# Attention and a routed feed-forward layer on one core: the last stage begins with the first chunk's norms, turn and routing ahead of the next chunks' work

## The reference

```python
def _L0_ffn_ref(x, Wr, br, W1, b1, W2, b2):
    scores0 = x[:, 0, :] @ Wr + br
    _, idx = jax.lax.top_k(scores0, k)
    W1g, b1g = (W1[idx], b1[idx])
    W2g, b2g = (W2[idx], b2[idx])
    h = jnp.einsum('bsd,bkde->bkse', x, W1g) + b1g[:, :, None, :]
    h = jax.nn.gelu(h, approximate=False)
    o = jnp.einsum('bkse,bkef->bksf', h, W2g) + b2g[:, :, None, :]
    return jnp.sum(o, axis=1) / k
x = L0_attn_x
x = x + _layernorm(_L0_attn_ref(_layernorm(x, axis=-1), ...), axis=-1)
x = x + _layernorm(_L0_ffn_ref(_layernorm(x, axis=-1), ...), axis=-1)
```

## Time and profile before

| | us |
|---|---|
| median of 3 runs | 2064.71 |
| lowest and highest run | 2061.21, 2065.99 |
| the profiled execution, its own time | 2067.85 |
| its span, first to last instruction | 2066.1 |
| stage C within the span | from 1706 to 2066.1 |
| busy over the span: PE, DVE, ACT, POOL | 1978.9, 1799.9, 1362.3, 316.4 |

### The profile page before, as it was taken

One profiled execution on the slowest core, in us unless ns is written; L12 is line 12 of the kernel. 1 busy time (PEld: TensorE's weight loads), 2 busy tenths in 40 slices (PEclk: granted clock), 3 DMA queues, 4 the chain that ended last, 5 costly groups with the idle time before them and its releaser, 6 DMA issues.

```text
span 2066.1 us, 39584 instructions
## 1 busy us (share of the span) xinstructions
PE 1978.9 (96%) x15700; PEld 863.7 (42%) x15700; DVE 1799.9 (87%) x3564; ACT 1362.3 (66%) x1651; POOL 316.4 (15%) x366
## 2 busy tenths in 40 slices
PE   6999999999999999999999999999999996999997
PEld 3655333333333333333333333333333324666664
DVE  6876799999999999999999999999899917899873
ACT  3766657777777777777777777777777781333332
POOL 5333201010110101011100101011010104322000
PEclk9999989999999999999999999999999998999998
DMA  4877613150504224030513314050422034453220
GB/s 124 254 242 207 156 26 67 28 90 8 89 18 85 47 48 82 16 89 13 85 32 68 71 26 89 7 90 20 82 48 50 17 104 108 123 148 108 82 67 31
DMA packets 144651, 162.40 MB, mean 79 GB/s; under 512 B 52690, under 2 KB 118354, under 8 KB 144466
## 3 DMA queue, kind: packets, MB, share of 16 engines
q1 hardware_dynamic: 137554, 147.26, 30.5%
q0 software_dynamic: 6912, 12.61, 2.7%
HBM read 99.77 MB, written 59.77 MB: 77 GB/s over the span
## 4 chain that ended last, share of the span: by engine, by line
PE 79%; DVE 13%; ACT 4%; issue 1%; SPq 1%; DMA 1%; POOL 0%; ACTq 0%; DVEq 0%; POOLq 0%
PE b_psO L1103 25%; PE b_psS L1086 25%; PE b_ring L605 13%; PE a_psQK L888 6%; DVE b_pmax L621 3%; PE a_psV L900 3%; PE c_psH L1483 3%; PE c_psO L1496 2%; ACT b_prob L1050 2%; PE b_ring L603 1%; DVE c_attn L105 1%; DVE c_ln_f_stats L81 1%; DVE c_ln_x_stats L81 1%; PE c_psA L1453 1%; DVE c_x L1314 1%
## 5 line engine op out<-in xcount | busy, mean ns | idle before, releaser
L621 DVE TENSOR_REDUCE b_pmax<-b_ring 128x1 f32<-128x512 f32 (+4 forms) x2284 | 1336.6, 647 | 82.1 <-PE b_ring L605 65.1
L1050 ACT ACTIVATE b_prob<-b_psS 128x1024 f32<-128x1024 f32 (+3 forms) x1280 | 1085.1, 895 | 372.2 <-PE b_psS L1086 367.5
L1086 PE MATMUL b_psS<-g_qT,g_kT 64*128 64x512 bf16 (+6 forms) x5120 | 837.5, 349 | 10.0 <-ACT b_prob L1050 7.2
L605 PE MATMUL b_ring<-g_kT,g_qT 64*128 64x512 bf16 (+2 forms) x2500 | 717.5, 349 | 4.0 <-DVE b_pmax L621 2.6
L1103 PE MATMUL b_psO<-b_prob,g_v 128*32 128x512 f32 (+3 forms) x5120 | 597.3, 542 | 0.3
L1086 PEld LDWEIGHTS b_psS<-g_qT,g_kT 64*128 64x128 bf16 (+1 forms) x5120 | 296.6, 94 | 462.9 <-ACT b_prob L1050 343.4
L1021 POOL TENSOR_SCALAR_AFFINE_SELECT b_prob<-b_prob 128x512 f32<-128x512 f32 x256 | 164.5, 643 | 1321.1 <-ACT b_prob L1050 1320.9
L605 PEld LDWEIGHTS b_ring<-g_kT,g_qT 64*128 64x128 bf16 x2500 | 221.7, 94 | 236.3 <-DVE b_pmax L621 163.7
L603 PE MATMUL b_ring<-later,query_of 64*128 64x128 bf16 x988 | 192.4, 220 | 1.9 <-DVE b_pmax L621 1.3
L1103 PEld LDWEIGHTS b_psO<-b_prob,g_v 128*32 128x32 f32 x5120 | 103.6, 108 | 174.2 <-issue 132.8
L1483 PE MATMUL c_psH<-c_yT,c_w1e 128*128 128x512 f32 x256 | 121.0, 618 | 20.8 <-ACT c_hT L1408 20.7
(11 more groups left out here) (113 smaller groups left out, 1059.4 us busy)
## 6 DMA issues: line engine op xcount, KB each, us to landing
qk_parts<-a_parts SPq DMA_DIRECT2D x64, 384.0 KB, 4.6
g_qT<-qk_parts SPq DMA_DIRECT2D x184, 128.0 KB, 3.9
g_kT<-qk_parts SPq DMA_DIRECT2D x184, 128.0 KB, 5.2
out_sums<-b_outT SPq DMA_DIRECT2D x64, 256.0 KB, 2.6
v_ones<-a_v SPq DMA_DIRECT2D x16, 544.0 KB, 6.0
g_v<-v_ones SPq DMA_DIRECT2D x32, 272.0 KB, 5.3
a_x<-in_L_attn_x SPq DMA_DIRECT2D x16, 512.0 KB, 4.8
c_x<-in_L_attn_x SPq DMA_DIRECT2D x16, 512.0 KB, 6.9
```

The costliest lines, as they stand in the source:

```text
L605: ins_ = self.nc.tensor.matmul(to, groups.qT[own, g, h // 2, 0, t * P:(t + 1) * P], groups.kT[own, g, h // 2, 0, pc * CH:pc * CH + w], sta ...
L621: self.nc.vector.tensor_reduce(pmax[:, c % 2].rearrange("p (h t) n -> p h t n", t=TT)[:, heads[0]:heads[-1] + 1:2, qt, pc], bank[:, 0:k * ...
L1050: nc.scalar.activation(prob[:, j % PBUF, 2 * s:2 * s + 2, off:CH], psS[:, 2 * s:2 * s + 2, off:CH], ACT.Exp).then_inc(exp_done, 1)
L1086: ins_ = nc.tensor.matmul(psS[:, 2 * s + p, off:CH], kT[own, g, s, ab, kt * P:(kt + 1) * P], qT[own, g, s, ab, c * CH + off:(c + 1) * CH], ...
```

## The change

The four filling steps are gone for PE, DVE, ACT and SP, and the first part of stage C is written out for each of them (`begin`). DVE brings chunk 0 through `take_projection`, `add_attention` and `normalise_x1` before it inverts the last row sums and takes chunk 1; `route(0)` comes after `take_projection` of chunk 1, then follow add and normalise of chunk 1, take, add and normalise of chunk 2, and the take of chunk 3. PE turns chunk 0 between its projection and that of chunk 1, scores after the projection of chunk 1, and does `hidden` of chunk 0 before the projection of chunk 3. Projection 2, and no longer only 3, waits for `idx_done`. ACT takes `gelu` of chunk 0 before `root_x1` of chunk 2. From `add_attention` of chunk 3 on, everything is as before. The number of instructions is the same.

```diff
@@ -1215,17 +1215,12 @@
         def steps(eng, step):
-            for c in range(NC):
-                step(-1, c)
             for b in range(B):
                 for c in range(NC):
                     step(b, c)
         def to_route(b, c):
-
-            if isinstance(b, int) and b == -1:
-                return 0 if c == NC - 2 else None
             return b + 1 if c == NC - 1 and not (isinstance(b, int) and b == B - 1) else None
         @block.sync
@@ -1252,21 +1247,26 @@
             def step(b, c):
                 new = ahead(b, c, 4)
-                if isinstance(b, int) and b == -1 and c == 1:
-                    chunks.store_inverses(sp, NPAIR - 1)
-                if new and not (isinstance(b, int) and new[2] < 2):
+                if new:
                     sp.wait_ge(x1_done, new[2] - 1)
                     chunks.load_x(sp, new[2], new[1] % 2)
                 if to_route(b, c) is not None:
                     load_experts(to_route(b, c))
-                if ahead(b, c, 0):
-                    n = b * NC + c
-                    sp.wait_ge(out_done, n + 1)
-                    sp.dma_start(out_t[bass.ds(n, 1)].rearrange("a p t d -> p (a t) d"), out_sb[:, c % 2]
-                                 ).then_inc(stored[c % 2], 16)
+                n = b * NC + c
+                sp.wait_ge(out_done, n + 1)
+                sp.dma_start(out_t[bass.ds(n, 1)].rearrange("a p t d -> p (a t) d"), out_sb[:, c % 2]
+                             ).then_inc(stored[c % 2], 16)
+
+            def load_next_x(n):
+                sp.wait_ge(x1_done, n - 1)
+                chunks.load_x(sp, n, n % 2)
             chunks.load_sums(sp, NPAIR - 1)
+            chunks.store_inverses(sp, NPAIR - 1)
+            load_next_x(2)
+            load_experts(0)
+            load_next_x(3)
             steps(sp, step)
             for p in range(2):
                 sp.wait_ge(stored[p], 16 + 16 * B * NC // 2)
@@ -1274,7 +1274,7 @@
         @block.gpsimd
         def _(pool):
             def step(b, c):
-                new = ahead(b, c, 4)
+                new = ahead(b, c, 4) if b >= 0 else (0, c, c)
                 if new:
                     b, c, n = new
                     if not (isinstance(n, int) and n < NC):
@@ -1292,6 +1292,8 @@
                     nc.gpsimd.tensor_tensor(cc[:, c], cc[:, c], inv[:, c], ALU.mult
                                             ).then_inc(cc_done, 1)
+            for c in range(NC):
+                step(-1, c)
             steps(pool, step)
         @block.vector
...
+            def begin():
+
+                take_projection(0, 0, 0)
+                add_attention(0, 0, 0)
+                normalise_x1(0, 0, 0)
+                chunks.invert_sums(v, NPAIR - 1)
+                take_projection(0, 1, 1)
+                route(0)
+                add_attention(0, 1, 1)
+                normalise_x1(0, 1, 1)
+                take_projection(0, 2, 2)
+                add_attention(0, 2, 2)
+                normalise_x1(0, 2, 2)
+                take_projection(0, 3, 3)
+
             def step(b, c):
-                first = isinstance(b, int) and b == -1
-                if first and c == 1:
-                    chunks.invert_sums(v, NPAIR - 1)
                 for k, part in ((2, normalise_x1), (1, route), (3, add_attention), (0, experts_end),
-                                (4, take_projection), (2, route)):
+                                (4, take_projection)):
                     which = ahead(b, c, k)
+                    if b == c == 0 and part is normalise_x1:
+                        continue
                     if part is route:
-                        if to_route(b, c) is not None and (k == 2) == first:
+                        if to_route(b, c) is not None:
                             route(to_route(b, c))
                     elif which:
                         part(*which)
@@ -1395,6 +1411,7 @@
             v.wait_ge(bias_summed, 1)
             nc.vector.tensor_tensor(consts.bo[:, :], psO[:, 0], consts.bo[:, :], ALU.add).then_inc(o_read, 1)
             v.wait_ge(o_read, 1)
+            begin()
             steps(v, step)
         @block.scalar
...
+                    if which and not (b == c == 0 and part is gelu):
                         part(*which)
             act.sem_inc(gelu_done, 2)
+            for c in range(2):
+                root_attn(0, c, c)
+                root_x1(0, c, c)
+                copy_y(0, c, c)
+            root_attn(0, 2, 2)
+            gelu(0, 0, 0)
+            root_x1(0, 2, 2)
             steps(act, step)
@@ -1446,7 +1470,7 @@
             def project(b, c, n):
                 pe.wait_ge(cc_done, n + 1)
                 wait_for(pe, a_read, n)
-                if c == 3:
+                if n == 2 or c == 3:
                     pe.wait_ge(idx_done, b + 1)
                 for t in range(TT):
                     for k in range(KD):
@@ -1466,7 +1490,7 @@
             def score_experts(b, n):
                 pe.wait_ge(yT_done, n + 1)
-                pe.wait_ge(a_read, n + 3)
+                pe.wait_ge(a_read, n + 3 if b > 0 else 2)
                 for k in range(KD):
                     ins_ = nc.tensor.matmul(psA[0:1, 0, 0:E], yT[:, k, 0, 0:1], wr[:, k],
                                             start=(k == 0), stop=(k == KD - 1))
@@ -1497,21 +1521,31 @@
                                                 start=(i == 0), stop=(i == 2 * KD - 1))
                 ins_.then_inc(o_done, 1)
+            def begin():
+                project(0, 0, 0)
+                turn_y(0, 0, 0)
+                project(0, 1, 1)
+                score_experts(0, 0)
+                project(0, 2, 2)
+                turn_y(0, 1, 1)
+                hidden(0, 0, 0)
+                project(0, 3, 3)
+                outer(0, 0, 0)
+
             def step(b, c):
-                first = isinstance(b, int) and b == -1
-                order = ((0, hidden), (1, score_experts), (0, outer), (2, turn_y), (4, project))
-                if first:
-                    order = ((4, project), (2, turn_y), (2, score_experts))
-                for k, part in order:
+                for k, part in ((0, hidden), (1, score_experts), (0, outer), (2, turn_y), (4, project)):
                     which = ahead(b, c, k)
+                    if b == c == 0 and part in (hidden, outer):
+                        continue
                     if part is score_experts:
-                        if to_route(b, c) is not None and (k == 2) == first:
+                        if to_route(b, c) is not None:
                             score_experts(to_route(b, c), to_route(b, c) * NC)
                     elif which:
                         part(*which)
             pe.wait_ge(consts.loaded, 16 * consts.LOADS)
             sum_bias(pe)
+            begin()
             steps(pe, step)
```

More of the change, by code:

```diff
@@ L1430, in step @@
                     which = ahead(b, c, k)
-                    if which:
+                    if which and not (b == c == 0 and part is gelu):
                         part(*which)
             act.sem_inc(gelu_done, 2)
+            for c in range(2):
[5 more added lines that the diff above has]
+            root_x1(0, 2, 2)
             steps(act, step)
```

## The result

The changed kernel takes 2074.52 us, the median of 6 runs (2071.15 to 2076.21), against 2064.6 for before (6 runs, 2058.71 to 2067.07): ratio 1.0041, 95% interval 1.0022 to 1.0059. Timed again later it was 1.0032 (1.0017 to 1.0046). It is slower, by 8.5 and 6.6 us by these ratios (9.9 and 7.7 by the differences of the medians); 6.4 had been forecast.

A forecast was written before the change was run, and what follows sets the result against it. DVE's opening of stage C was taken to set when the full pipeline starts. Gelu start 0.1, normalise 1.51, take 3.85 and chunk 6's multiplication 0.9 sum to 6.4 us, on 2064.71 giving 2071.1; range 2064.5 to 2074.0.

The forecast's parts named there:

- the old wait behind the gelus: DVE's idle time until ACT, busy with chunk 0's gelus, gives a root: 4.44 us before, forecast to stay at 3.5.
- the start of the gelus: ACT's first gelu of chunk 0: forecast at 1753.9, 0.1 us later than before.
- the tail: End of the opening on DVE: normalise_x1 of chunk 2 and chunk 3's take now follow the gelus, 1.51 and 3.85 us.
- the mark: DVE's start of add_attention of chunk 3, 1760.58 before; all engine lists are the same from there; forecast 6.4 us late.
- chunk 4's multiplication: On POOL, forecast to fall in DVE's add of chunk 1 and stretch it by 1.7 us.
- the take with its root: DVE's take_projection of chunk 3 plus a root, forecast to follow normalise_x1 of chunk 2 and cost 3.85 us.
- the multiplication of chunk 6: On POOL, forecast to fall where DVE has no gap and cost 0.9 us more, bounds 0.3 and 1.6.
- nothing is given back: Claim that later steps keep their order and the 6.4 us delay stays to the end.
- The loop of gelu and hidden: Rival: this loop on ACT and PE sets the pace and absorbs DVE's delay; 1.6 us earlier, 2063.1; 12 in 100.
- PE was not warm for projection 1: Rival, denied here: turn and projection 1 run at 2.4 GHz, 4.5 us instead of 7.4; 2068.2; 12 in 100.
- The transfers: Rival: expert loads collide with chunk 5's load, so hidden and the gelus start some 3 us later; 2074.1; 8 in 100.
- the prediction's other reckoning: By the skill's exclusion rule, chunk 4's multiplication costs up to 2.1 us anywhere in DVE's add; sum 6.8 instead of 6.4.

The follow-up runs named there:

- p1_first: The changed kernel with PE doing the projection of chunk 1 ahead of the turn of chunk 0; ratio to before 1.0002 (0.9985 to 1.0019).
- new_tail: The changed kernel with the opening of before (three projections first, route after the take of chunk 2); ratio to before 1.0025 (1.0014 to 1.0036).
- kept_warm_all: The changed kernel with 44 added PE matmuls: 25 before the turn of chunk 0, 9 before projection 2, 10 behind it; ratio to before 1.0011 (0.9994 to 1.0029).
- new_opening: The changed kernel with the order of before from hidden of chunk 0 to the take of chunk 3; ratio to before 1.0022 (1.0011 to 1.0033).
- early_route: Against before: route ahead of chunk 2's take, first scores in psO, gelus of chunk 0 ahead of chunk 2's root; ratio to before 0.9988 (0.9975 to 1.0002).
- kept_warm: The changed kernel with 20 added PE matmuls between projection 0 and the turn of chunk 0; ratio to before 1.0035 (1.0019 to 1.0051).

## Why the prediction was right, and where not

**The direction and the mechanism held.** Idle time moved forward to projection 1, the old wait behind the gelus stayed, and the earlier route brought nothing: it ended 2.8 us sooner (2.4 forecast) and the gelus were not earlier. The p1_first run shows the first of these as a cause by itself, 6.0 us, and it is the one that my sum did not name as a term: there it was buried in the start of the gelus. The new_tail run shows the same for the tail, which the sum did name.

**The range.** It went from 2064.5 to 2074.0. The forecast's base of 2064.71 times 1.0041 is 2073.2, within it near its upper end, and times 1.0032 it is 2071.3. The median of the changed kernel as it was timed, 2074.52, lies 0.5 above it.

**The terms of the sum, at the mark.** Start of the gelus: 0.1 later than before was forecast, 1.0 measured. What moved it: DVE's wait for turn and projection 1 was 0.5 shorter than worked out, chunk 4's multiplication cost 2.06 instead of 1.7, and ACT waited 0.91 for hidden. This last is the term that was missing: I let hidden of chunk 0 follow "at about 1748 as before", at the full clock, though with the 1.7 of the multiplication my own times leave PE idle for some 2 us between projection 2 and the turn of chunk 1. It was idle for 2.39, and turn and hidden ran mostly at the 1.2 GHz level. Normalise 1.51 and the take with its root 3.85 came as forecast, and the multiplication of chunk 6 added 2.17 to the take. Less the 0.54 that it had cost before (L105 at 1760.80 took 1.92 instead of 1.38) that is 1.6, the upper end of my 0.3 to 1.6, where I took 0.9. Together 8.5 at the mark, or 8.0 as the sum counts it, against 6.4. The 3.5 us that I left of the old wait were 1.82: I had left out the root ahead of the add of chunk 2 (0.45), and the multiplication of chunk 5 stretched that add by 2.04. Neither moved the mark.

**After the mark** the forecast was that nothing is given back. In the two pairs of profiles the whole stage is 9.1 and 7.9 us longer and the timed losses are 8.5 and 6.6 us (0.41 and 0.32% of 2065), so that holds for the full change within what the scatter of the clock leaves to see. As a rule it is not shown: the marks of new_opening, new_tail and kept_warm_all are 7.9, 7.7 and 6.4 late, the timed losses only 4.5, 5.2 and 2.3. What gives the time back there, and whether chance helped the full change to keep its loss, stays open.

**The rivals.** The loop of gelu and hidden did not absorb the delay. PE was not warm for projection 1; kept_warm_all prices that rival at 2.1, not 2.9. The transfers did not hold up hidden in the changed kernel, but by a small margin: the last bias load, issued at 1739.15, took 6.6 us to land (2.8 at most in before), some 0.6 ahead of the start of hidden at 1746.37. They did hold it up in four of the experiments, by 1.6 to 5.3 us.

**The shared port.** The Trainium skill, SBUF — State Buffer, practical consequences, has DVE instructions with two SBUF inputs exclude a GpSimd instruction that reads SBUF. L86, 128x4 with two SBUF inputs, took 2.32 beside the multiplication and agrees; L1304, which reads one input from PSUM, and L81 ran beside one without loss in p1_first, which agrees as well. L1316, which adds two SBUF inputs and is the prediction's L1314, is held too. Where POOL began first, L1316 took 3.38 instead of 1.23 (kept_warm_all) and 3.26 (early_route). DVE and POOL of kept_warm_all:

```profile
1749.22 3.38 DVE L1316 TENSOR_TENSOR c_x<-c_x,c_attn 128x1024 f32<-128x1024 f32 x1
...
1749.17 2.34 POOL L1292 TENSOR_TENSOR c_cc<-c_cc,c_inv 128x1024 f32<-128x1024 f32 x1 [8.63 <-DMA c_inv<-inverse_sums]
```

In kept_warm L1316 began first, at 1749.26, and kept its 1.23, and the multiplication of 1749.84 took 2.86 instead of 2.34. So the prediction's other reckoning, in which L1314 is held as well, was the right one; here the multiplication fell on L105 and cost 2.06. Most of the cost in these kernels is on that line, whose instructions read one tensor; no row shows why they are held.

## What to carry to other kernels

When one item's chain is put first to shorten a latency, look at which independent work of the other engines now stands behind it in a strictly ordered list: here one projection behind one transpose turned 6 us of full overlap into a wait, and swapping these two took the loss back, 6.0 us of it by the wait itself and 2.8 by the luck of where POOL's multiplications then fell. Before moving the producer of a gate, write down everything that the gate waits for; an input that comes 2.8 us sooner is worth nothing while another of its inputs is as late as ever. And price an engine's next stretch by how long it will have idled, not by what the same rows took when it had not.

## What was not expected of the hardware

The clock of PE was back at the 1.2 GHz level after a wait of 2.4 us in both executions of the changed kernel (turn of chunk 1), and after waits of 2.55 to 2.58 us in some executions and not in others, with the same program (3.70 or 5.30 to 5.40 us for one half of hidden); a filler that ended 2.46 us ahead of the turn saved 0.5 us, one that ended 0.31 ahead saved 2.2. A POOL multiplication of 2.3 us cost DVE from nothing to 2.2 us, depending on which DVE instruction it met, which of the two began first and how much of them overlapped.
